# Six transformer layers on one core: a floor taken by a maximum over pairs, a last feature tile of 128 rows, and new orders of the work

## The reference

```python
# shift_tokens: the second half of the features comes from the token before
q, k, v = split(shift_tokens(x) @ Wqkv)              # 16 heads of 64
q = q / maximum(norm(q), 1e-12) * q_scale            # the floor; same for k
q, k = rotate(q), rotate(k)                          # position tables
sim = q @ k.T * 8, masked to windows of 64 and the window before
x = softmax(sim) @ v @ Wo + x
xn = layernorm(shift_tokens(x)) * g + b
a, gate = split(xn @ W1 + b1)                        # 682 features each
x = (a * gelu(gate)) @ W2 + b2 + x
```

## Time and profile before

| | |
|---|---|
| median of 3 runs | 3378.83 us (3373.56 to 3382.44) |
| the profiled execution | 3374.63 us |
| its span | 3373.1 us |
| mean granted TensorE clock | 0.966 |

### The profile page before, as it was taken

One profiled execution on the slowest core, in us unless ns is written; L12 is line 12 of the kernel. 1 busy time (PEld: TensorE's weight loads), 2 busy tenths in 40 slices (PEclk: granted clock), 3 DMA queues, 4 the chain that ended last, 5 costly groups with the idle time before them and its releaser, 6 DMA issues. The chain is left out here.

```text
span 3373.1 us, 80406 instructions
## 1 busy us (share of the span) xinstructions
PE 3120.3 (93%) x30032; PEld 2752.0 (82%) x30032; DVE 2772.4 (82%) x5013; ACT 2521.9 (75%) x7047; POOL 1923.5 (57%) x1536
## 2 busy tenths in 40 slices
PE   4888797289999999999999999999999999999997
PEld 3666565268998989998989988999899998989896
DVE  2368788688889998889988899888998889998883
ACT  1687687178777787777878778878788877887774
POOL 4446644565556565656565656565665656565651
PEclk8898897699999999999999999999999999999998
DMA  3111100110000100000100011000100000100000
GB/s 121 57 35 35 57 7 7 35 32 29 2 2 20 32 30 2 2 11 27 44 2 2 2 36 35 11 2 2 30 24 28 2 2 20 32 29 8 5 8 26
DMA packets 27777, 75.03 MB, mean 22 GB/s; under 512 B 4120, under 2 KB 9848, under 8 KB 27256
## 3 DMA queue, kind: packets, MB, share of 16 engines
q1 hardware_dynamic: 22224, 52.63, 5.0%
q0 software_dynamic: 4864, 16.78, 1.6%
q10 hardware_dynamic: 304, 0.47, 0.1%
HBM read 65.68 MB, written 4.19 MB: 21 GB/s over the span
## 5 line engine op out<-in xcount | busy, mean ns | idle before, releaser
L1571 POOL TENSOR_TENSOR turned<-by_cos,turned 128x512 f32<-128x512 f32 x384 | 493.7, 1286 | 987.8 <-DVE turned L2021 987.8
L1829 ACT ACTIVATE prob<-ps_s,ebias,rnorm 128x128 f32<-128x128 f32 x1536 | 681.8, 459 | 13.7 <-DVE ebias L2041 11.7
L1575 POOL TENSOR_TENSOR rnorm<-norm,half 128x8 f32<-128x8 f32 x384 | 645.0, 1680 | 41.0
L1838 ACT ACTIVATE prob_t<-ps_t 128x512 f32<-128x512 f32 x384 | 230.1, 599 | 315.9 <-PE ps_t L1661 311.2
L2015 DVE TENSOR_TENSOR by_cos<-ps_qk,cos_t 128x512 f32<-128x512 f32 x384 | 264.9, 690 | 121.5 <-ACT sq L1802 119.4
L1598 PE MATMUL ps_qk<-w_hi,x_hi 128*128 128x512 f32 x768 | 328.4, 428 | 18.6 <-DVE x_lo L2005 13.7
L1737 PE MATMUL ps_f<-hid_hi,w_hi 128*128 128x256 f32 (+1 forms) x1056 | 318.1, 301 | 8.3 <-DVE hid_lo L2095 8.2
L2029 DVE TENSOR_SCALAR norm<-norm 128x8 f32<-128x8 f32 x384 | 311.5, 811 | 13.2
L2034 DVE TENSOR_REDUCE negmax<-ps_s 128x8 f32<-128x1024 f32 x192 | 233.9, 1218 | 107.2 <-PE ps_s L1652 107.1
L1829 ACT ACTIVATION_READ_ACCUMULATOR prob<-ps_s,ebias,rnorm 128x1 f32 x1536 | 316.2, 206 | 0.0
L1598 PE MATMUL ps_qk<-w_hi,x_lo 128*128 128x512 f32 x768 | 305.1, 397 | 0.0
(11 more groups left out here) (284 smaller groups left out, 9925.0 us busy)
## 6 DMA issues: line engine op xcount, KB each, us to landing
w_raw<-in_w_qkv SPq DMA_DIRECT2D x24, 768.0 KB, 4.8
w_raw<-in_w SPq DMA_DIRECT2D x12, 693.0 KB, 4.0
w_raw<-in_w_o SPq DMA_DIRECT2D x12, 512.0 KB, 3.4
w_raw<-in_w SPq DMA_DIRECT2D x6, 768.0 KB, 4.3
x_tok<-in_x SPq DMA_DIRECT2D x8, 256.0 KB
kept<-x_t SPq DMA_DIRECT2D x8, 256.0 KB, 2.0
w_raw<-kept SPq DMA_DIRECT2D x8, 256.0 KB, 3.0
out<-rows_out SPq DMA_DIRECT2D x8, 256.0 KB, 2.9
```

Source lines behind the costliest of these rows:

```text
L1571: G.tensor_tensor(turned[:, k, :], by_cos[:, :], turned[:, k, :], ALU.add).then_inc(s["turned"], 1)
L1575: G.tensor_tensor(rnorm[:, i % RR, :], norm2[:, k, :], half[:, :], ALU.pow).then_inc(s["rnorm"], 1)
L1829: last = A.activation(prob[:, k, h, :], half_bank(h % 2, k)[:, T(h // 2)], ACT.Exp, bias=ebias[:, i // NU % 2, k, h:h + 1], scale=rnorm[:, ...
```

## The change

1. The floor. The sum of squares goes to the even columns of `sum2` (8 pairs), whose odd columns hold 1e-24 since the start, and the floor is a maximum over each pair (a reduction, 8 results of 16 values) into `norm2`; it was a maximum with a constant in place.
2. The last tile of features. `w_2_mm` has two products with 128 rows for it in place of three with 42. The spare rows 64 to 105 now hold a second copy: of a and gate (DVE reads them too: four instructions for two), and of the weights, with `w2_lo` holding in rows 0 to 63 the high part and in rows 64 to 127 the low part. So `w2_lo` x `hid_hi` gives hi x hi and lo x hi at once. `w2_high` is three instructions (1280, 256 and 256 columns) for one of 1536, `w2_low` two for one, and a copy of zeros into rows 64 to 127 of `w2_hi` stands once ahead of the first `take_x`.
3. The memory clears on POOL ahead of the layers cover less.
4. New lists of order and offsets on POOL, PE, ACT and DVE.

The core of the diff. Of the lists one line stands for each of POOL, ACT and DVE: on ACT the exponentials also go from t-3 to t-4 and `attend` from 7 to 8, so that the copy of unit t-2 and the exponentials of unit t-4 open a step; on DVE `gate_value(q, 1)` stood at 23.

```diff
-        G.memset(x1[:, :, :], 0.0).then_inc(s["lset"], 1)
+        G.memset(x1[:, :, ::PAD], 0.0).then_inc(s["lset"], 1)
...
-            for i in units(t, 2):
+            for i in units(t, 3):
                 rotated(i)
...
-                r = slice(0, width(j))
-                for n, (w, x) in enumerate(((w2_hi, hid_hi), (w2_lo, hid_hi), (w2_hi, hid_lo))):
-                    last = E.matmul(ps_f[0][:, mt * N:(mt + 1) * N], w[r, j, T(mt)].bitcast(F32R),
-                                    x[r, j, :].bitcast(F32R), start=j + n == 0, stop=j == NJ - 1 and n == 2)
+                terms = ((w2_hi, hid_hi), (w2_lo, hid_hi), (w2_hi, hid_lo)) if j < NJ - 1 else ((w2_lo, hid_hi), (w2_hi, hid_lo))
+                for n, (w, x) in enumerate(terms):
+                    last = E.matmul(ps_f[0][:, mt * N:(mt + 1) * N], w[:, j, T(mt)].bitcast(F32R),
+                                    x[:, j, :].bitcast(F32R), start=j + n == 0, stop=j == NJ - 1 and n == 1)
...
-            A.activation(flat(w2_hi).bitcast(F32R), raw(NJ * D), ACT.Copy).then_inc(s["high"], 1)
+            A.activation(flat(w2_hi)[:, 0:(NJ - 1) * D].bitcast(F32R), raw((NJ - 1) * D), ACT.Copy)
+            A.activation(w2_hi[0:REST, NJ - 1, :].bitcast(F32R), raw(NJ * D)[0:REST, (NJ - 1) * D:], ACT.Copy)
+            A.activation(w2_lo[:, NJ - 1, :].bitcast(F32R), raw(NJ * D)[:, (NJ - 1) * D:], ACT.Copy).then_inc(s["high"], 1)
...
-            V.tensor_reduce(norm2[:, k, :], sq[:, :].rearrange("p (h d) -> p h d", d=DH), AX.X, ALU.add
-                            ).then_inc(s["norm2"], 1)
+            if i:
+                V.wait_ge(s["norm2_floor"], i)
+            V.tensor_reduce(sum2[:, :, 0], sq[:, :].rearrange("p (h d) -> p h d", d=DH), AX.X, ALU.add).then_inc(s["norm2"], 1)
             V.wait_ge(s["norm2"], i + 1)
-            V.tensor_scalar(norm2[:, k, :], norm2[:, k, :], 1e-24, None, ALU.max).then_inc(s["norm2_floor"], 1)
+            V.tensor_reduce(norm2[:, k, :], sum2[:, :, :], AX.X, ALU.max).then_inc(s["norm2_floor"], 1)
...
-            for i in units(t, 1):
+            for i in units(t, 2):
                 flip_qk(i)
...
+            for q in passes(t, 25):
+                gate_value(q, 1)           # DVE; at 23, late in the step, before
```

More of the change, by code:

```diff
@@ L1780, in pe @@
                 w_o_mm(q, 1)
[L1781 to L1784, removed]
+            for q in passes(t, 21):
+                hidden_mm(q, 3)
+            for q in passes(t, 21):
+                hidden_mm(q, 4)
             for q in passes(t, 20):
                 hidden_mm(q, 2)
[L1787 to L1792, removed]
     def act():
@@ L1907, in act @@
         for t in range(STEPS):
+            for i in units(t, 4):
+                soften(i)
             for q in passes(t, 20):
                 hidden_read(q, 0)
-            for layer in layers(t, 11):
-                w_o_high(layer, 0)
+            for i in units(t, 2):
+                flip_qk(i)
+            for q in passes(t, 23):
+                hidden_hi(q, 0)
+            for q in passes(t, 19):
+                linear_hi(q)
+            for r in groups(t, 8):
+                attend(r)
             for q in passes(t, 21):
                 hidden_read(q, 1)
-            for q in passes(t, 24):
-                hidden_hi(q, 0)
+            for q in passes(t, 21):
+                hidden_read(q, 2)
+            for layer in layers(t, 9):
+                w_o_high(layer, 0)
+            for q in passes(t, 22):
+                gelu(q, 0)
+            for q in passes(t, 25):
+                hidden_hi(q, 1)
             for i in units(t, 0):
                 project(i)
[L1918 to L1921, removed]
             for i in units(t, 5):
                 flip_prob(i)
[L1924 to L1933, removed]
-            for i in units(t, 1):
-                flip_qk(i)
-            for layer in layers(t, 14):
+            for layer in layers(t, 16):
                 w1_high(layer, 0)
@@ L1939, in act @@
                 w1_high(layer, 1)
-            for layer in layers(t, 12):
+            for layer in layers(t, 10):
                 w_o_high(layer, 1)
+            for q in passes(t, 17):
+                square(q)
             for layer in layers(t, 20):
                 w2_high(layer)
-            for q in passes(t, 18):
-                linear_hi(q)
+            for q in passes(t, 22):
+                gelu(q, 1)
     def dve():
@@ L2135, in dve @@
         split_wqkv(0, 0)
+        V.tensor_copy(w2_hi[REST:P, NJ - 1, :].bitcast(F32R), hidden[REST:P, NJ - 1, :])
         for t in range(STEPS):
+            for layer in layers(t, -2, 1):
+                split_wqkv(layer, 0)
+            for layer in layers(t, 4):
+                split_wqkv(layer, 2)
+            for layer in layers(t, 12):
+                w_o_low(layer, 1)
+            for layer in layers(t, 22):
+                w2_low(layer)
+            for q in passes(t, 0):
+                take_x(q)
@@ L2137, in dve @@
             for q in passes(t, 23):
                 hidden_read(q, 5)
-            for q in passes(t, 0):
-                take_x(q)
-            for q in passes(t, 20):
-                linear_lo(q)
-            for layer in layers(t, 12):
-                w_o_low(layer, 0)
             for r in groups(t, 4):
                 soften(r)
+            for i in units(t, 1):
+                rotate(i)
+            for q in passes(t, 16):
+                add_x(q)
+            for layer in layers(t, 0):
+                tables(layer)
@@ L2147, in dve @@
+            for i in units(t, 5):
+                weigh(i)
+            for q in passes(t, 25):
+                gate_value(q, 1)
+            for layer in layers(t, 5):
+                split_wqkv(layer, 3)
             for q in passes(t, 23):
                 gate_value(q, 0)
[L2149 to L2156 removed]
+            for q in passes(t, 19):
+                normalise(q)
@@ L2157, in dve @@
+            for q in passes(t, 27):
+                new_state(q)
+            for q in passes(t, 18):
+                take_spread(q)
             for layer in layers(t, 1):
                 split_wqkv(layer, 1)
-            for i in units(t, 5):
-                weigh(i)
+            for layer in layers(t, 9):
+                w_o_low(layer, 0)
+            for layer in layers(t, 19):
+                w1_low(layer, 1)
+            for layer in layers(t, 17):
+                w1_low(layer, 0)
```

98 lines of the change are left out of this document (42 added, 56 removed).

## The result

The changed kernel takes **3345.66 us** (median; 3341.73 to 3355.77, 4 runs), the kernel before 3380.64 on the same chip: ratio **0.9904, 95% interval 0.9876 to 0.9932**. The forecast was 3343. The profiled execution took 3341.73 us with a span of 3340.3, 32.8 us shorter than the span of before. The number was right; the experiments show that several of the steps that gave it were not, and that their errors cancelled.

A forecast was written before the change was run, and what follows sets the result against it. PE's own instructions were taken to set the time in 46 of 48 passes. -38.4 + 4.4 - 2 + 1.0 + 0.3 + 4 - 3 = -33.7 us gave 3340.9 or 3345.1, said as 3343; range 3324 to 3362.

The forecast's parts named there:

- w_2: End of w_2_mm on PE: 0.40 us gained 96 times, 38.4 us in all; 11.5 if row changes cost nothing.
- Additional reads: DVE's four reads of the last tile: 0.95 us a pass, below what the floors leave; +1.0 us in the last pass.
- attend ahead of score: PE's order: shape changes cost nothing, within 17 us; scores 1.10 us later, hidden in full passes; +4.4 us in the first.
- Rival (d): Copy to qk_t behind the second gelu: ACT late for scores, PE waits 1.5 us a pass, +72, 3415 us; chance 0.10.
- The floor: DVE's L2029, 811 ns to about 0.17 us: worth nothing in a full pass, -2 us in the first steps.
- rival (a): DVE's next product waits beside POOL's sum and holds back POOL's power: 14 us, the floor's 2 lost, 3359; chance 0.15.
- Other new orders: Moved units on POOL, PE and ACT: PE finds its inputs as before; the copy to qk_t fits by 0.1 to 0.3 us.
- No new line above 5 us: Among PE's waits: the changed kernel would show no new line above 5 us.
- the two small terms for weights (+4 - 3): w2_high in three pieces delays the copy to qk_t, +4 us (0 to 8); shorter wait for lin_lo, -3 (0 to -4).
- The last stretch: Last pass, where all stand in a chain: the two more DVE reads cost +1.0 us.

The follow-up runs named there:

- the room alone: Kernel before with an unused buffer of 16 columns, every buffer behind it 64 bytes further on, old floor kept: ratio 0.9968, pass 54.74 us.
- old orders with the three products of 128 rows: Kernel before with the new floor and three products of 128 rows for the last w_2 tile, single reads: 3322.57 us, ratio 0.9846.

## Why the prediction was right, and where it was not

**w_2.** The cause was right, and the kernel with three products of 128 rows shows it. The size was low: 0.40 us a group, measured 0.51 (1.01 us a pass), as the earlier trace rows ends where the products begin that are slow as well.

**Additional reads: the step that failed.** I set 0.95 us of reads against the time that the floors leave on VectorE, and so at nothing in a full pass. But the reads begin when TensorE's last hidden product ends, whatever VectorE had to do before, and two chains hang on their end: gate_value, rotate, the next projection, which has nothing in hand; and gelu, exponentials, the copy to qk_t, the scores, with 0.23 us. Either gives back 0.8 to 1.0 us a pass. A share of busy time was used where the chain behind one wait counted.

**attend ahead of score.** The borders sum to nothing, as said (the three distances of the earlier trace rows only change places). But the swap is not worth nothing: it is what makes room on the second chain. Without it the pass is 54.77 us and the gain gone. The copy's margin, said to be 0.1 to 0.3 us, came out at 0.35. Rival (d) thus named the right place, and what I held against it, ScalarE's idle fifth, was no argument: the idle 0.84 us lies ahead of the very gelu that is late. Once, ahead of the first mean, the swap costs 8.5 us and not 4.4.

**The floor.** Expected: 2 us and nothing in a full pass. In the old orders its form does give nothing there, and rival (a)'s contention was real. The Trainium skill ("SBUF — State Buffer", Who interferes with whom) says that a VectorE instruction with two inputs in SBUF contends with a GpSimd instruction that reads SBUF, and a reduction does not. Here the trace agrees: the product goes from 723 to 976 ns on VectorE, the power from 1680 to 2053 on GpSimd, and the floor takes 170 ns beside POOL's sum. Its price on the path was nil in the old orders and not 14 us: the kernel with the floor and the one with the room alone have the same pass, 54.74. What the sum lacked there is the move of the buffers by 64 bytes, 0.245 us a pass, 12 us in 48. In the new orders "worth nothing in a full pass" failed outright: DVE's reads are on the path, and the part is worth 0.42 us a pass, 0.24 of it in waits. The room alone was not tried in the new orders, so that the lighter floor is what takes these waits away is read from the timelines and not shown by itself.

**Other new orders.** Costed at nothing but for a few us. Beside the other two parts they are worth 23.3 us in the layers (2695.9 to 2672.6), and by themselves they cost 47. In a full pass they bring a wait of 0.25 us a pass ahead of w_o, about 0.1 us more at borders, and beside it 1.3 to 1.4 us for hid_lo in six passes; against old orders with the three products of 128 rows, they lose. "No new line above 5 us" was wrong: hid_lo went from 4.9 to 14.0 us and rotate from 4.9 to 10.8; the two small terms for weights (+4 - 3) came out at about +2. The last stretch fell by 3.4 us where +1.0 was forecast.

In sum, against the forecast's terms and with the sizes that w_2 and the room have in the old orders: 10 us more from w_2, 12 us from the place of the buffers and 2 to 4 in the last stretch stood against 12 for the wait ahead of w_o, 5 at borders, 3 to the first mean, 3 in the front and 1 in passes with weights. The doubled reads and the cover for them came to nothing together, and I had counted neither. That the span came out 32.8 us shorter where 33.7 was forecast is luck. This split is one of several: the parts act on each other, and in the changed kernel itself w_o's groups shrink by 0.06 us a pass and not by 0.105.

Open: what about the buffers' places makes products faster (only two places were tried), and why VectorE's read or copy ahead of w_o is late by 0.25 us under the new orders (with the score first, where TensorE comes 0.88 us later in a pass, it is not). That the contention alone makes L2055 and the power longer was not tried apart from the form of the floor.

## What to carry to other kernels

Work that is added behind a wait is paid from the end of that wait: follow every chain that hangs on it to the bounding engine, and compare with its slack in the trace, never with busy time. Test a change's parts alone and in pairs before crediting them: here the parts sum to +38 us and the whole to -36, and the floor is worth 17 us by itself and 31 beside the other two. And when a change declares a buffer, run it once with the buffer alone.

## What the hardware showed that was not expected

- 64 bytes of unused room ahead of the moving buffers: 0.32% (ratio 0.9968), with distances in w_o from 0.120 to 0.118 us. Room behind attn_lo leaves w_o and speeds w_2, more than the room ahead of all (4.506 us a pass for 4.567), though w_2's own moving buffers stand at the same place in both.
- Products of 42 rows also slow what comes behind them: eight variance products with one column from 0.700 to 0.803 us in all, those that spread rstd from 0.330 to 0.436.
- More rows made TensorE faster: with three products of 128 rows in place of three of 42 a group costs 0.37 us less (0.75 us a pass), with what comes behind it.
